# A gated cross-attention block on one core: Wq loaded in halves from both queues, warming products of one broadcast column, and one more batch's inverse deviations sent through DRAM

## What is computed

```python
# x, ctx: (8, 256, 256); Wq, Wk, Wv: (256, 256); w_gate, w_up: (704, 256); w_down: (256, 704)
q = layernorm(x) @ Wq.T;  k = ctx @ Wk.T;  v = ctx @ Wv.T
scores = where(causal, q @ k.T / 16, -inf)
probs = softmax(scores, axis=queries)
x = x + tanh(g_xattn) * (probs @ v)
xq = fake_quant(layernorm(x))              # one scale: the largest |value| of the whole tensor
h = fake_quant(silu(xq @ Qg.T) * (xq @ Qu.T))   # again one scale for the whole tensor
x = x + tanh(g_ffn) * (h @ Qd.T)
```

## Time and profile before

| | |
|---|---|
| time, median of 3 runs | 109.54 us (109.43 to 109.54) |
| the profiled execution: its own time | 109.32 us |
| the profiled execution: its span | 107.4 us |
| PE busy | 99.9 us (93%) |
| DVE busy | 81.6 us (76%) |
| ACT busy | 69.6 us (65%) |
| POOL busy | 44.2 us (41%) |
| DMA | 12.18 MB, mean 113 GB/s |

### The profile page before, as it was taken

How to read it: one execution, slowest core, us unless ns; L and a number is a source line. 1 busy time by engine, 2 the same in 40 slices (tenths; PEclk the granted TensorE clock), 3 DMA queues, 4 the chain that set the end, 5 groups by cost and what they waited for, 6 DMA issues and landing times.

```text
span 107.4 us, 1812 instructions
## 1 busy us (share of the span) xinstructions
PE 99.9 (93%) x600; PEld 76.8 (71%) x600; DVE 81.6 (76%) x212; ACT 69.6 (65%) x131; POOL 44.2 (41%) x80
## 2 busy tenths in 40 slices
PE   5989999999999999999999987999999699999960
PEld 2268888988989897988988973444433398788850
DVE  0275296597899979868678978649999997869990
ACT  0422252567882817457677978889988899999800
POOL 7215035065371817343192593065578540520000
PEclk9999999999999999999999999999999999999999
DMA  3999999999001411305000000000000000005547
GB/s 28 383 384 260 386 419 422 410 406 395 31 23 26 33 16 14 38 1 57 0 0 0 0 0 0 6 0 3 0 0 0 0 6 0 0 0 195 195 148 249
DMA packets 5769, 12.18 MB, mean 113 GB/s; under 512 B 1280, under 2 KB 2048, under 8 KB 5760
## 3 DMA queue, kind: packets, MB, share of 16 engines
q1 hardware_dynamic: 5184, 11.28, 31.8%
q10 hardware_dynamic: 576, 0.79, 2.1%
HBM read 9.96 MB, written 2.10 MB: 112 GB/s over the span
## 4 chain that ended last, share of the span: by engine, by line
PE 52%; ACT 18%; DVE 17%; issue 4%; DMA 4%; ACTq 1%; DVEq 0%
PE ps L457 13%; PE ps L479 11%; PE ps L497 10%; ACT ints L890 7%; DVE shared L1124 5%; DVE hmax L1129 4%; ACT xn L801 4%; DMA wq_sb<-in_wq 4%; PE ps L650 3%; PE ps L507 3%; PE ps L509 2%; PE ps L508 2%; PE ps L554 2%; ACT silu L863 2%; PE ps L669 2%
## 5 line engine op out<-in xcount | busy, mean ns | idle before, releaser
L650 PE MATMUL ps<-xq,wguT 128*128 128x512 bf16 x80 | 17.7, 379 | 0.8 <-DVE xq L1104 0.8
L428 POOL TENSOR_TENSOR shared<-up_sb,silu 128x1024 f32<-128x1024 f32 x5 | 11.8, 2365 | 9.7 <-ACT up_sb L868 9.7
L650 PEld LDWEIGHTS ps<-xq,wguT 128*128 128x128 bf16 x80 | 7.6, 98 | 10.6 <-DVE shared L1124 1.1
L457 PE MATMUL ps<-wvT,shared 128*128 128x256 f32 x56 | 13.3, 380 | 0.0
L479 PE MATMUL ps<-shared,a_sb 128*128 128x256 f32 x56 | 13.2, 379 | 0.0
L1129 DVE TENSOR_REDUCE hmax<-shared 128x1 f32<-128x2048 f32 (+1 forms) x6 | 12.7, 2108 | 0.6
L863 ACT ACTIVATE silu<-ps,gu_scale 128x1024 f32<-128x1024 f32 x10 | 11.1, 1115 | 2.5 <-PE ps L650 2.5
L744 ACT ACTIVATE probs<-neg_scores,neg_max 128x256 f32<-128x256 f32 x8 | 4.1, 508 | 12.7 <-DVE neg_max L941 12.5
L497 PE MATMUL ps<-uT,shared 128*128 128x256 f32 (+1 forms) x64 | 11.9, 329 | 0.0
L457 PEld LDWEIGHTS ps<-wvT,shared 128*128 128x128 f32 x56 | 10.6, 190 | 1.6 <-issue 0.2
L497 PEld LDWEIGHTS ps<-uT,shared 128*128 128x128 f32 x64 | 10.7, 190 | 1.2
(11 more groups left out here) (131 smaller groups left out, 200.0 us busy)
## 6 DMA issues: line engine op xcount, KB each, us to landing
shared<-in_xc SPq DMA_DIRECT2D x6, 512.0 KB, 10.6
out<-xn SPq DMA_DIRECT2D x7, 256.0 KB, 2.0
xs<-in_x SPq DMA_DIRECT2D x3, 512.0 KB, 8.3
shared<-in_wgu SPq DMA_DIRECT2D x3, 512.0 KB, 7.7
shared<-in_xc SPq DMA_DIRECT2D x4, 256.0 KB, 6.0
wd<-in_wd SPq DMA_DIRECT2D x1, 768.0 KB, 10.2
r_wide<-spread SPq DMA_DIRECT2D x4, 128.0 KB, 4.0
wq_sb<-in_wq ACTq DMA_DIRECT2D x1, 256.0 KB, 3.9
```

What stands on the lines that cost most here:

```text
L428: nc.gpsimd.tensor_tensor(hid[:, 2 * i + 1, :], up_sb[i % 2][:], silu1[i % 2][:], ALU.mult).then_inc(hid_done[1], 1)
L457: last = nc.tensor.matmul(bank2(VB[b])[:, k, :], ctxT(b)[:, e, k * P:(k + 1) * P], weights[:, e, :], start=(e == 0), stop=(e == KT - 1))
L650: last = nc.tensor.matmul(bank(4 * half + 2 * g + c), wguT[:, i, g, k, :], xq[:, k, col:col + CH], start=(k == 0), stop=(k == KT - 1))
```

## The change

- `WIDE_FROM` goes from 4 to 3: batch 3's inverse deviations go through DRAM as well. PE's two transposes and ACT's copy for batch 3 go. The two DMAs for it are issued by ACT, not SP: the write behind `values_out(0)`, the read behind `quantise_weights(0)`, each with its wait ahead of it on ACT.
- Wq is loaded in two halves, the first thing on each queue, each with its semaphore. Wk is SP's second load.
- `xT(0)` is loaded in halves too, one on each queue, behind the context and `wvT`. x of batch 1 moves from SP's fourth load to ACT's fifth.
- `dense` shrinks from 128x512 to one column, and the warming products read it as a broadcast.
- `spread_deviation(1)` moves on PE from ahead of `scores(0)` to behind it.

```diff
-WIDE_FROM = 4
+WIDE_FROM = 3
-        dense = sb("dense", [P, CH], BF16)
+        dense = sb("dense", [P, 1], BF16)
+        def everywhere(n):
+            return spread[n].rearrange("p t -> (p t)").unsqueeze(0).to_broadcast([P, P * QT])
...
+            sp.dma_start(wq_sb[:, 0], wq_in[:, 0]).then_inc(wq_here[0], 16)
             sp.dma_start(wk_sb[:], wk_in).then_inc(wk_here, 16)
-            sp.dma_start(xT(0), xc_in[0, :, 1]).then_inc(xT_here[0], 16)
             sp.dma_start(ctxT(0), xc_in[0, :, 0]).then_inc(c_here[0], 16)
-            load_x(1)
-            sp.dma_start(xT(1), xc_in[1, :, 1]).then_inc(xT_here[1], 16)
+            sp.dma_start(xT(0)[:, 0], xc_in[0, :, 1, 0]).then_inc(xT0_here[0], 16)
+            sp.dma_start(xT(1), xc_in[1, :, 1]).then_inc(xT1_here, 16)
...
-                    nc.tensor.matmul(bank(bk), dense[:, 0:P], dense[:], start=True, stop=True)
+                    nc.tensor.matmul(bank(bk), dense[:].to_broadcast([P, P]), dense[:].to_broadcast([P, CH]), start=True,
+                                     stop=True)
...
             values_tile(0, 1).then_inc(v_done, 1)
-            spread_deviation(1)
 
             for b in range(LAST - 1):
                 scores(b)
+                if b == 0:
+                    spread_deviation(1)
                 project_queries(b + 1)
...
-            act.dma_start(wq_sb[:], wq_in).then_inc(wq_here, 16)
+            act.dma_start(wq_sb[:, 1], wq_in[:, 1]).then_inc(wq_here[1], 16)
             act.dma_start(xs[:, 0:QT, :], x[:, 0:QT, :]).then_inc(x_here[0], 16)
             act.dma_start(wvT[:], wvT_in).then_inc(wv_here, 16)
+            act.dma_start(xT(0)[:, 1], xc_in[0, :, 1, 1]).then_inc(xT0_here[1], 16)
+            act.dma_start(xs[:, QT:2 * QT, :], x[:, QT:2 * QT, :]).then_inc(x_here[1], 16)
...
                 exponentials(b)
                 values_out(b)
+                if b == 0:
+                    act.wait_ge(rstd1_done, WIDE_FROM + 1)
+                    act.dma_start(spread[0], rstd1[:, WIDE_FROM]).then_inc(first_spread_out, 16)
...
                     quantise_down_weights(0)
+                if b == 0:
+                    act.wait_ge(first_spread_out, 16)
+                    act.dma_start(r_wide[:, 0].rearrange("q p t -> q (p t)"), everywhere(0)).then_inc(r_wide_here[0], 16)
...
-            dve.wait_ge(wq_here, 16)
             for h in range(KT):
+                dve.wait_ge(wq_here[h], 16)
```

More of the change, by code:

```diff
@@ L190, in down_half @@
             return bank2(c - 1)[:, t, :]
-        wq_here = sem("wq_here")
+        wq_here = [sem(f"wq_here{h}") for h in range(KT)]
         wk_here = sem("wk_here")
@@ L198, in gated_block @@
         c_here = [sem(f"c_here{b}") for b in range(2)]
-        xT_here = [sem(f"xT_here{b}") for b in range(2)]
+        xT0_here = [sem(f"xT0_here{e}") for e in range(KT)]
+        xT1_here = sem("xT1_here")
         xc_here = [sem(f"xc_here{b}") for b in range(2, B)]
@@ L223, in gated_block @@
         spread_out = sem("spread_out")
+        first_spread_out = sem("first_spread_out")
         r_wide_here = [sem(f"r_wide_here{b}") for b in range(WIDE_FROM, B)]
@@ L329, in _ @@
             load_xc(7)
-            for b in range(WIDE_FROM, B):
+            for b in range(WIDE_FROM + 1, B):
                 n = b - WIDE_FROM
@@ L334, in _ @@
                 sp.dma_start(spread[n], rstd1[:, b]).then_inc(spread_out, 16)
-                sp.wait_ge(spread_out, 16 * (n + 1))
-                everywhere = spread[n].rearrange("p t -> (p t)").unsqueeze(0).to_broadcast([P, P * QT])
-                sp.dma_start(r_wide[:, n].rearrange("q p t -> q (p t)"), everywhere).then_inc(r_wide_here[n], 16)
+                sp.wait_ge(spread_out, 16 * n)
+                sp.dma_start(r_wide[:, n].rearrange("q p t -> q (p t)"), everywhere(n)).then_inc(r_wide_here[n], 16)
             for c in range(STEPS - 1):
@@ L473, in project_queries @@
                 if b == 1:
-                    pe.wait_ge(xT_here[b], 16)
+                    pe.wait_ge(xT1_here, 16)
                 else:
@@ L560, in _ @@
             values_tile(0, 0)
-            pe.wait_ge(xT_here[0], 16)
             for f in range(KT):
                 for e in range(KT):
+                    pe.wait_ge(xT0_here[e], 16)
                     pe.wait_ge(a_ready, e + 1)
```

## The result

The changed kernel takes 112.09 us (111.20 to 112.98, 4 runs) against 109.54 (109.43 to 109.64). The ratio is 1.0206, 95% interval 1.0131 to 1.0281: slower by 2.1%, where 0.4% faster was forecast. The profiled execution took 111.69 us with a span of 109.8, so it is 2.37 above the profiled one of before.

A forecast was written before the change was run, and what follows sets the result against it. PE's joined work was taken to bound the kernel. The terms -0.64 + 0.23 - 0.22 + 0.15 = -0.48 from the median give 109.06; 109.05 us was predicted, range 108.6 to 109.5.

The forecast's parts named there:

- The bound: Whole kernel: PE's work, joined end to end from 5.84 to 56.48, sets the time; starting sooner shortens it one for one.
- Wq in halves, a gain of 0.64: Start: Wq lands at 3.9, PE starts at 5.2 behind Wk; gain 0.64 us, bounds 0.5 and 0.75.
- x of batch 1, a loss of 0.23: ACT's fifth load lands at 8.95 instead of 8.3, scores start at about 11.0; loss 0.23 us, bounds 0 and 0.5.
- The next loads, hidden: Start: `wvT` at 6.85 for values wanted at 7.0, hidden by 0.15; halves of `xT(0)` hidden by 0.3.
- The broadcast column, 0.4 of cover: Warming products run from 0.87 to 5.12, ahead of PE's start; with the old memset 0.4 of the gain would be lost.
- Batch 3's transposes, a gain of 0.22: PE loses two transposes of batch 3 on the chain; gain 0.22 us.
- The write, L about 4.0 and a loss of 0.15: ACT's wait for batch 3's write, of length L, ahead of batch 1's exponentials; loss 0.15 us, bounds 0 and 0.55.
- The formula: ACT late by d = 17.4 + L + 0.4 - 21.62 = L - 3.8; PE waits d less about 0.15.
- the upper bound of 4.5: Batch 3's write under load was put between 2.8 and 4.5 us from issue to landing, nearer the upper end.
- The rival that had this mechanism at L = 5.3: Write slow under load: PE waits 1.35 us at L = 5.3, giving 110.25 us; chance 12%.
- The read back, hidden: Batch 3's read, 5.5 us, lands at 27.3, wanted by DVE's scaling at 28.7; hidden by 1.4.
- The second rival: The start gives little: x of batch 1 at 9.3 or later, `wvT` late, write costs 0.55; 109.45 us; chance 11%.

The follow-up runs named there:

- the kernel with the old loads: Changed kernel with batch 3 back on PE, `xT(0)` loaded whole and x of batch 1 back on SP's queue; 109.41 us, ratio 0.9975.
- batch 3 on PE: Changed kernel without ACT's two DMAs and their waits, `WIDE_FROM` at 4 again; 109.17 us, ratio 0.9959; run again 109.18 us, ratio 0.9948.
- the kernel in which the engines were partly idle: Changed kernel with SP holding back its loads to two issued and not landed; 121.19 us, ratio 1.0885.
- only batch 3 through DRAM: Kernel before with one part alone: batch 3's inverse deviations through DRAM, both DMAs issued by ACT; 112.34 us, ratio 1.0231.
- the kernel with the unused read: Changed kernel with batch 3 back on PE, plus one unused ACT read of 128 rows of 8 bytes from DRAM to SBUF; 108.89 us, run once.

## Why the prediction was wrong

1. **The bound.** Right. PE's work, joined end to end, sets the time up to 56.5, and a wait put into it comes out at the end: 2.26 us at the hand-over, 2.37 in the time.
2. **Wq in halves, a gain of 0.64.** Right in mechanism and size up to PE's first product in this execution, which gained 0.68, with some luck: Wq released DVE 1.19 sooner, at 3.48 (forecast 0.7, 3.9), but Wk, landing behind it, set PE's start at 5.16 (forecast 5.2). In twelve profiles the gain lies between 0.24 and 0.72; the bounds were 0.5 and 0.75. The other size for Wq, an estimate of 0.60 by the fit in the Trainium skill (DMA: Bandwidth & Descriptors, Anatomy of one DMA), was further from the 1.19 than the 0.73 of the rows; the page gives this fit for DMAs that GpSimd issues, and these are SP's and ACT's.
3. **x of batch 1, a loss of 0.23.** Mis-sized. It landed at 9.46, not 8.95. The scores started at 11.21 instead of 11.0, and behind the moved transposes PE began the queries of batch 1 at 12.84 instead of 12.94: 0.10 left of the 0.41. The estimate counted the bytes on both queues and took them as evenly shared; the kernel with the old loads suggests that the place in ACT's queue mattered as much as they did.
4. **The next loads, hidden.** Not quite: the values started at 7.23 instead of 7.0, and `wvT` landed at 7.1 (5.5 us after its issue at 1.64) instead of 6.85.
5. **The broadcast column, 0.4 of cover.** The warming starts at 0.88, as forecast, but the full tile in its place costs nothing in these runs (0.9938 against 0.9959 and 0.9948). In its profiled execution the ten products ended at 5.11, since they took 3.81 us, and Wk set the start at 5.18. At 4.25 us they would have ended at 5.55, where Wk lands in some executions (5.60 in batch 3 on PE). So the 0.4 is neither confirmed nor excluded for every execution.
6. **Batch 3's transposes, a gain of 0.22.** It was there: nothing of them is on the chain.
7. **The write, L about 4.0 and a loss of 0.15.** This is the step that failed. L was 6.87. The formula was right. The start was 0.09 early by the last transposes ahead of the attention (18.03 against 18.12), instead of 0.41, so ACT is late by 24.75 - 21.94 = 2.81, and PE by 0.15 less, 2.66; PE's `attend(1)` started at 26.96, against 24.62 - 0.22 - 0.09 = 24.31, which is 2.65. The sum is then -0.10 - 0.22 + 2.65 = 2.33, and 2.37 was measured. What was wrong is the upper bound of 4.5. It is SP's slowest write, 3.5, plus the 1.0 us by which the scalars landed behind `wvT` in the same queue. The same row gives 6.4 us from issue to landing for the scalars, a small transfer on ACT's queue beside the loads. I took the 5.4 us up to `wvT`'s landing as waiting for `wvT`; no row of before shows a small transfer that starts on an idle queue beside the loads, so none bounded L at 4.5. The write on ACT's idle queue took 6.87. The rival that had this mechanism at L = 5.3 was given 12%. The estimate beside it from the Trainium skill (DMA: Bandwidth & Descriptors, Latency and other measured facts), 1.8 us more under load, pointed the right way and was also too small: the loads added 3.7 to 4.0. The trace bears out its direction, not its size.
8. **The read back, hidden.** Right: 4.9 us from issue to landing (forecast 5.5), wanted much later now.

The second rival's sum names 0.55 for the write and adds 0.3; as added it gives 109.48, not 109.45. That changes nothing in the outcome.

What stays open is why a transfer of 1 KB takes 6.9 us beside the loads. It is not the direction. The number of rows explains 1.6 us of it, and 2.6 us of the rest pass before its first packet moves; what holds this packet is not shown. A version in which SP's queue pauses completely for the write was not tried.

## What to carry to other kernels

When a wait for a DMA goes into the program of a computing engine, ask what stands behind it in that program and when it is wanted. The bound for the round trip has to come from a transfer that started under the same traffic: here the same 1 KB took 3 us in quiet and 7 us beside loads at 400 GB/s. Issue such a transfer early, and put the wait at the last place before its result is needed; moving the second wait behind the next batch's exponentials and values took back the whole loss of 2.7 us by the medians, though four of ten executions stayed some 1 us above the others. And a gain at the start has to be followed through each load that comes behind it, since the next one that is late takes it back.

## What the runs showed of the hardware

- A small transfer on ACT's queue beside SP's loads takes 6.6 to 8.7 us from issue to landing (6.87, 7.0, 7.2, 6.9, 6.6, 8.7 in six kernels), against 2.9 and 3.2 without them; 16 rows take 5.3, a read of 128 rows 6.5. The 8.7 belongs to the kernel in which the engines were partly idle. Beside loads at 400 GB/s its first packet moves 3.4 us after the issue, without them 0.8.
- PE's clock fell to its lower level behind the wait in some executions. The windows of "only batch 3 through DRAM", from where PE runs dry to the clock's return (us, busy of PE, PEld, DVE, ACT and POOL, PEclk, DMA share, GB/s):

```profile
24.00:27.50 3.50, 1.05 (x5) 0.57 (x3) 0.80 (x3) 1.52 (x6) 1.09 (x2) 1.00 1.03 331
27.50:31.00 3.50, 3.10 (x8) 2.53 (x9) 1.77 (x7) 3.20 (x7) 0.89 (x2) 0.51 0.39 106
```

PE had been idle for 2.85 us. When it came back at 27.90 it ran at half of the clock, 1.2 GHz, until about 31. In the changed kernel's profiled execution, with 2.49 us of idle time, it did not. That makes such a wait dearer in some executions than its own length. The mean granted clock of every execution bears this out for the longest ones: 0.985 at 114.07 and 114.22 us of "only batch 3 through DRAM", 0.993 to 1.00 at its other four (111.48 to 112.58), and 0.985 at 112.98 of the changed kernel, 1.00 at its other three. What spreads those three from 111.20 to 112.50 is not shown.
- The moment at which PE's clock comes up at the start differs from execution to execution: within the warming products (ten in 3.81 us with the full tile, in 3.96 with the column in the kernel with the unused read), at their end (4.2), or only within the products with Wk (2.4 to 2.6 us instead of 1.98).
